# Turning the uint8 codes of x by a transposing DMA in tiles 10 to 15, with the statistics of x one tile further ahead

## The chip, the cores and the metric

The kernel runs on one core of a Trainium2 chip. The metric is the device time of one execution in microseconds (us), the median of several runs. Five engines work side by side: TensorE (PE, matmuls and transposes into PSUM), VectorE (DVE), ScalarE (ACT), GpSimd (POOL), and SyncE (SP), which here only issues transfers. Each takes its own instructions strictly in program order; they meet through semaphores.

## The reference

x has 2 batches of 1024 rows of 2048 floats, the context 2 batches of 2048 by 2048. Cut to what matters:

```python
def fake_quant(x, scale, zp):
    q = clip(round(x / scale + zp), 0, 255)
    return (q - zp) * scale
def attn(x1, x2):                       # x1 = layernorm(x), x2 = ctx
    return matmul(fake_quant(x1, s1, z1), fake_quant(x2, s2, z2))
def lora_moe(f, A, B, Wr):              # 4 experts of rank 16, top 2
    logits = f @ Wr.T
    gates = softmax(keep_top2(logits))
    mid = einsum('tf,erf->ter', f, A)
    return sum_e(gates[e] * (mid[e] @ B[e].T)) * 4.0
x = x + tanh(g_xattn) * attn(layernorm(x), ctx)
x = x + tanh(g_ffn) * lora_moe(layernorm(x), A, B, Wr)
```

## The kernel before

The 2048 rows of x are 16 tiles of 128 rows, numbered 0 to 15 here and in the code. For each tile the kernel does this:

- **Codes of x.** DVE takes mean and variance of x (`stats_x` twice, each two `bn_stats` of 512 columns and each waiting for its half of x from HBM; then `var_x`). POOL raises the variance to -1/2 (`power_x`), DVE makes scale and offset from it (`scale_of_x`), ACT writes the codes as bytes (`scale_x` to `x_byte`). PE turns them in byte pairs, as eight 128x128 transposes of 2-byte values into the PSUM bank `ps_gate` (`turn_q1`); ACT spreads them to fp16 less the zero point (`copy_q1T` to `q1T`, two buffers in turn). In the second batch ACT also sums the codes of each row (`sum_codes`), and DVE makes a correction of the sum (`shift_of_row`).
- **Main product.** `main(b, n)` is 16 matmuls of 128x128 by 128x512 for quarter n of the 2048 columns. DVE adds each quarter to x (`add_main`, which gives x1) and takes its statistics (`stats_h`, then `var_h`, POOL's `power_h`, DVE's `bias_h`). There are two PSUM banks for the quarters, so that main(b, 1) waits until `add_main(b-1, 3)` has emptied its bank.
- **Second layer norm, in two fp16 parts.** ACT writes the high part of h (`high_part`) and h itself (`normal_half` twice), POOL the low part (`low_part` twice). Both parts are turned, and PE multiplies them with A and Wr (`mid_hi` twice, `mid_lo` twice). In tiles 8 to 13 (`MOVED`) the turning is done by SP with transposing transfers of 128x1024 fp16 (`move_hi`, `move_lo`), in the others by PE.
- **Gates and delta.** DVE ranks the four logits (`rank_gates`, which waits for the last `mid_lo`), ACT takes the exponentials (`gate_exp`), DVE makes the gated products (`weigh`), PE turns them into `ps_gate` (`turn_gate`), DVE splits them into two parts (`split_gate`), and PE makes the four quarters of delta, two matmuls each (`delta`). DVE adds them (`add_delta`), SP stores the rows.

Each engine's order is written out by hand up to tile 8. From tile 9 (`STEADY`) on a loop over b runs on each engine. Iteration b holds the main product of tile b, the second layer norm of tile b-1, and gates and delta of tile b-2. For x the loop before works on tile b+1. The last instructions ahead of the loop are those of tile 8's third and fourth quarter and of the gates of tile 7.

x lies in a ring of five tiles. `load_x(b+3)` is issued when tile b-2 is stored. The lines of the four `load_x` of tiles 10 and 11 stand just ahead of the loop on SP, behind the stores of tile 6.

Of the kernel before, what the change touches and what calls it, by code (L numbers as in the profile page):

```python
# [11 lines left out]
F16 = mybir.dt.float16  # L12
I32 = mybir.dt.int32
U8 = mybir.dt.uint8

P = 128
BANK = 512
# [10 lines left out]
RING = 5  # L28
FIRST = 4
STEADY = 9  # L30

MOVED = range(STEADY - 1, 14)
UNITS = 18
# [4 lines left out]
def build(nc, x, ctx_in, params, lora_a, lora_b, out):  # L38
# [21 lines left out]
    with ExitStack() as stack:  # L60
# [3 lines left out]
        def sem(name):  # L64
            return stack.enter_context(nc.semaphore(name))
# [141 lines left out]
        h_bias_ready, h2_ready, h_hi_ready, h_lo_ready = sem("h_bias_ready"), sem("h2_ready"), sem("h_hi_ready"), sem("h_lo_ready")  # L207
        hi_turned, hiT_ready = sem("hi_turned"), sem("hiT_ready")
        lo_turned, loT_ready = sem("lo_turned"), [sem("loT_ready0"), sem("loT_ready1")]
        hi_moved, lo_moved = [sem("hi_moved0"), sem("hi_moved1")], [sem("lo_moved0"), sem("lo_moved1")]  # L210
        last_hi = sem("last_hi")
        hi_used, lo_used, mids_read, mids_scaled = sem("hi_used"), sem("lo_used"), sem("mids_read"), sem("mids_scaled")
# [18 lines left out]
        def half(h):  # L231
            return slice(h * HALF, (h + 1) * HALF)
# [28 lines left out]


        loT = q1T[:, 3, :, :].rearrange("p (h k) m -> p h k m", h=2)
        c_byte = c_code[:, :, :].rearrange("p s n -> p (s n)").bitcast(U8).rearrange("p (s n two) -> p s n two", s=2, two=2)[:, :, :, 0]
        q2_byte = q2[:, 1, :, :].rearrange("p k n -> p (k n)").bitcast(U8).rearrange("p (k n two) -> p k n two", k=KT, two=2)
        q2_pair = q2[:, 1, :, :].rearrange("p k n -> p (k n)").bitcast(F32).rearrange("p (k n) -> p k n", k=KT)
# [10 lines left out]
        def _(sp):  # L277
# [27 lines left out]
            def move_hi(b, h):  # L305
                sp.wait_ge(h_hi_ready, b + 1)
                sp.wait_ge(hi_used, 2 * (b - 1) + h + 1)
                sp.wait_ge(lo_used, 2 * turned(b))
                sp.dma_start_transpose(hT[:, h, :, :], h_hi[:, half(h)]).then_inc(hi_moved[h], 16)

            def move_lo(b, h):
                sp.wait_ge(h_lo_ready, 4 * b + 2 * h + 2)
# [78 lines left out]
            load_x(11, 1)  # L391
            for b in range(STEADY, TILES):
                if b - 1 in MOVED:
                    move_hi(b - 1, 0)
                    move_hi(b - 1, 1)
                    move_lo(b - 1, 0)
                    store(b - 2, 0)
                    move_lo(b - 1, 1)
                    store(b - 2, 1)
                else:  # L400
                    for h in range(2):
                        store(b - 2, h)
                if b + 3 < TILES:
                    load_x(b + 3, 0)
                    load_x(b + 3, 1)
# [10 lines left out]
        def _(pool):  # L416
# [14 lines left out]
            def power_x(b):  # L431
                pool.wait_ge(x_var_ready, b + 1)
                nc.gpsimd.tensor_tensor(x_rstd[:, :], x_var[:, :], half_neg[:, :], ALU.pow).then_inc(x_rstd_ready, 1)  # L433
# [81 lines left out]
            power_h(7)  # L515
            low_part(7, 0)
            low_part(7, 1)
            for b in range(STEADY, TILES):
                power_h(b - 1)
                low_part(b - 1, 0)  # L520
                if b < LAST:
                    power_x(b + 1)
                low_part(b - 1, 1)
            power_h(LAST)


        @block.scalar
        def _(act):
# [16 lines left out]

            def scale_x(b):
                act.wait_ge(q_scale_ready, b + 1)
                wait(act, q1_turned, b)
                wait(act, codes_summed, 2 * (b - PER_B))
                nc.scalar.activation(x_byte[:, :], xr[:, b % RING, :], ACT.Identity,  # L550
                                     bias=q_scale[:, 1:2], scale=q_scale[:, 0:1]).then_inc(x_scaled, 1)
# [8 lines left out]
                                         accum_out=code_sums[:, h:h + 1]).then_inc(codes_summed, 1)  # L560

            def copy_q1T(b):
                act.wait_ge(q1_turned, b + 1)
                if b >= FIRST:
                    last_user = {FIRST: 0, FIRST + 1: 2}.get(b, b - 2)
                    act.wait_ge(main_done, parts_done(last_user, NB - 1))
                nc.scalar.activation(q1T_of(b).rearrange("p (j two) m -> p j two m", two=2),  # L567
                                     as16(turn_bank(b), U8).rearrange("p (j m two) -> p j two m", m=P, two=2),
                                     ACT.Identity, bias=neg_centre[:, 0:1], scale=1.0).then_inc(q1T_ready, 1)

            def high_part(b):
# [144 lines left out]
            for b in range(STEADY, TILES):  # L716
                if b > STEADY:
                    gate_exp(b - 2)
                high_part(b - 1)
                normal_half(b - 1, 0)  # L720
                normal_half(b - 1, 1)
                if b - 1 not in MOVED:
                    copy_hiT(b - 1, 0)
                    copy_hiT(b - 1, 1)
                if b < LAST:
                    scale_x(b + 1)
                if b - 1 not in MOVED:
                    copy_loT(b - 1)
                if b < LAST:
                    copy_q1T(b + 1)  # L730
                    sum_codes(b + 1)
                else:
                    gate_exp(b - 1)

# [13 lines left out]
        def _(pe):  # L748
# [152 lines left out]
            def program(general):  # L901
# [284 lines left out]
                for b in range(STEADY, TILES):  # L1186
                    main(b, 0, general)
                    if b == STEADY:
                        delta(b - 2, 0)
                        delta(b - 2, 1)  # L1190
                    main(b, 1, general, 0, 6)
                    if b > STEADY:
                        turn_gate(b - 2, b + 1)
                    main(b, 1, general, 6, 12)
                    if b > STEADY:
                        delta(b - 2, 0)
                        delta(b - 2, 1)
                    main(b, 1, general, 12)
                    if b - 1 not in MOVED:
                        turn_hi(b - 1, 0)  # L1200
                        turn_hi(b - 1, 1)
                    main(b, 2, general, 0, 10)
                    delta(b - 2, 2)
                    delta(b - 2, 3)
                    main(b, 2, general, 10, 12)
                    mid_hi(b - 1, 0)
                    if b - 1 not in MOVED:
                        turn_lo(b - 1, 0)
                    main(b, 2, general, 12)
                    mid_hi(b - 1, 1)  # L1210
                    if b - 1 not in MOVED:
                        turn_lo(b - 1, 1)
                    main(b, 3, general, 0, 2)
                    if b < LAST:
                        turn_q1(b + 1, b - 1)
                    main(b, 3, general, 2, 6)
                    if b - 1 not in MOVED:
                        mid_lo(b - 1, 0)
                        mid_lo(b - 1, 1)
                    main(b, 3, general, 6, 14)  # L1220
                    if b - 1 in MOVED:
                        mid_lo(b - 1, 0)
                        mid_lo(b - 1, 1)
                    main(b, 3, general, 14)
                    if b - 1 not in MOVED:
                        turn_gate(b - 1, TILES)
                delta(LAST - 1, 0)
                delta(LAST - 1, 1)
                pe.wait_ge(x1_ready, NB * LAST + 3)
# [9 lines left out]
                mid_lo(LAST, 0)  # L1239
                mid_lo(LAST, 1)  # L1240
                keep_busy(10)
                turn_gate(LAST, TILES)
                last_delta()

            with pe.If_ne(flag, 0):
# [8 lines left out]
        def _(dve):  # L1254
# [406 lines left out]
            add_main(8, 2)  # L1661
            weigh(7)
            stats_h(8, 2)
            for b in range(STEADY, TILES):
                if b > STEADY:
                    rank_gates(b - 2)
                else:
                    split_gate(b - 2)
                add_main(b - 1, 3)
                stats_h(b - 1, 3)  # L1670
                var_h(b - 1)
                if b > STEADY:
                    weigh(b - 2)
                bias_h(b - 1)
                if b < LAST:
                    stats_x(b + 1, 0)
                add_main(b, 0)
                if b > STEADY:
                    split_gate(b - 2)
                else:  # L1680
                    add_delta(b - 2, 0)
                shift_of_row(b)
                stats_h(b, 0)
                if b < LAST:
                    stats_x(b + 1, 1)
                    var_x(b + 1)
                if b > STEADY:
                    add_delta(b - 2, 0)
                add_delta(b - 2, 1)
                add_main(b, 1)  # L1690
                if b < LAST:
                    scale_of_x(b + 1)
                add_delta(b - 2, 2)
                add_delta(b - 2, 3)
                stats_h(b, 1)
                if b - 1 not in MOVED:
                    copy_loT(b - 1)
                add_main(b, 2)
                if b == LAST:
                    rank_gates(b - 1)  # L1700
                stats_h(b, 2)
                if b == LAST:
                    weigh(b - 1)
            split_gate(LAST - 1)
# [50 lines left out]
```

## Time and profile before

| what | value |
|---|---|
| median of 3 runs | 349.45 us (349.28 to 350.9) |
| the profiled execution | 350.64 us, of which its span is 348.9 us |
| PE busy | 321.4 us, 92% |
| DVE busy | 276.0 us, 79% |
| granted clock of TensorE | 1.00 of full speed |
| ACT busy | 252.2 us, 72% |
| POOL busy | 109.5 us, 31% |
| 52 loads of ctx, 32 of x | 14.8 us and 6.2 us from issue to landing (median) |

The span is the time from the first instruction to the last in the profiled execution. All starts are microseconds from its beginning. The busy share is a mean over a first part (to about 190 us, with the load of ctx beside it), the loop (iterations 9 to 15, about 199 to 325 us) and a tail. Times of PE come in two forms: the timeline gives when an instruction starts, the chain of waits when it takes over from the one before it, which is some 0.16 us later for matmuls in a row.

### The profile page before, as it was taken

What the parts mean: (1) busy time and instruction counts of PE and PEld (TensorE: products, weight loads), DVE (VectorE), ACT (ScalarE), POOL (GpSimd) and SP (SyncE); (2) the same over time, 40 slices, a digit from 0 to 9 for tenths busy, and PEclk for the clock granted to TensorE, in tenths of its full rate; (3) what the DMA queues carried; (4) which work ended last, traced back from release to release, by engine and by line L of the source; (5) the groups of instructions that cost most, each with busy time, mean ns of one, the idle gap of its engine ahead of it and who ended that gap; (6) DMA issues with size and microseconds to landing.
All of it is one profiled execution on the core that took longest, in us unless ns stands there. A gap on an engine that the chain in (4) does not pass through costs nothing.

```text
span 348.9 us, 6112 instructions
## 1 busy us (share of the span) xinstructions
PE 321.4 (92%) x2180; PEld 175.4 (50%) x2180; DVE 276.0 (79%) x695; ACT 252.2 (72%) x221; POOL 109.5 (31%) x123
## 2 busy tenths in 40 slices
PE   0389999999999999998999999999999999999884
PEld 0134444446675555544656546454545454556452
DVE  4798789988779869865877985969797887965885
ACT  1699899999999999888999347565565656566050
POOL 3100243226656270244235042232415050505000
PEclk9999999999999999999999999999999999999999
DMA  6999999931389858967330777464949491822023
GB/s 207 416 417 421 418 421 417 420 123 45 137 287 365 321 174 267 333 223 245 144 120 16 235 234 224 128 204 138 213 140 191 153 174 69 168 75 111 11 119 124
DMA packets 44528, 75.45 MB, mean 216 GB/s; under 512 B 27600, under 2 KB 27600, under 8 KB 44368
## 3 DMA queue, kind: packets, MB, share of 16 engines
q1 hardware_dynamic: 44496, 75.02, 63.3%
q8 instruction: 20, 0.33, 0.3%
q14 instruction: 12, 0.10, 0.1%
HBM read 51.94 MB, written 16.78 MB: 197 GB/s over the span
## 4 chain that ended last, share of the span: by engine, by line
PE 62%; DVE 14%; DMA 12%; issue 4%; ACT 3%; SPq 3%; POOL 1%; DVEq 0%; ACTq 0%; POOLq 0%
PE ps_main L785 32%; DMA out_x<-xr 5%; DMA xr<-in_x 4%; PE ps_delta L785 4%; PE ps_mid L844 4%; DMA q<-in_ctx 4%; PE ps_delta L874 3%; PE ps_turn L785 3%; PE ps_delta L876 3%; DVE xr L1360 3%; DVE small_tile L1304 2%; PE ps_mid L785 2%; PE ps_gate L785 2%; PE ps_mid L855 2%; PE ps_turn L829 2%
## 5 line engine op out<-in xcount | busy, mean ns | idle before, releaser
L785 PE MATMUL ps_main<-q,q1T 128*128 128x512 f16 x832 | 201.9, 379 | 2.8 <-DVE xr L1360 2.0
L785 PEld LDWEIGHTS ps_main<-q,q1T 128*128 128x128 f16 x832 | 76.1, 98 | 84.4 <-issue 8.6
L450 POOL TENSOR_TENSOR h_parts<-work,h_parts 128x512 f16<-128x512 f32 x30 | 34.2, 1161 | 54.4 <-ACT work L587 54.4
L581 ACT ACTIVATE h_parts<-xr,small_tile 128x2048 f16<-128x2048 f32 x15 | 31.4, 2091 | 25.7 <-DVE small_tile L1377 24.8
L550 ACT ACTIVATE x_byte<-xr,small_tile 128x2048 uint8<-128x2048 f32 x16 | 33.4, 2089 | 20.1 <-DVE small_tile L1319 20.1
L1304 DVE BATCH_NORM_STATS2 small_tile<-xr 128x6 f32<-128x512 f32 x64 | 40.8, 681 | 8.5 <-DMA xr<-in_x 8.5
L543 ACT ACTIVATE c_code<-q,small_tile 128x1024 uint8<-128x1024 f32 x32 | 38.1, 1237 | 9.2 <-DMA q<-in_ctx 8.6
L1365 DVE BATCH_NORM_STATS2 small_tile<-xr 128x6 f32<-128x512 f32 x64 | 43.7, 687 | 0.8
L1360 DVE SCALAR_TENSOR_TENSOR xr<-ps_main,small_tile,xr 128x512 f32<-128x512 f32 x52 | 38.5, 741 | 3.4 <-PE ps_main L785 3.4
L438 POOL TENSOR_TENSOR small_tile<-small_tile 128x1 f32<-128x1 f32 x16 | 8.8, 551 | 89.1 <-DVE small_tile L1373 89.1
L450 POOL TENSOR_TENSOR h_parts<-q1T,h_parts 128x512 f16<-128x512 f32 x30 | 34.3, 1164 | 2.1 <-ACT q1T L587 2.1
L874 PE MATMUL ps_delta<-lora_bT,gT_hi 128*128 128x512 f32 x60 | 30.0, 500 | 0.9 <-DVE gT_hi L1425 0.4
L567 ACT ACTIVATE q1T<-ps_gate,small_tile 128x2048 f16<-128x2048 uint8 x12 | 23.6, 1963 | 5.7 <-PE ps_gate L768 5.6
L433 POOL TENSOR_TENSOR small_tile<-small_tile 128x1 f32<-128x1 f32 x16 | 9.4, 590 | 51.0 <-DVE small_tile L1311 51.0
L756 PE MATMUL ps_main<-ident_h 128*128 128x512 f16 x47 | 13.3, 433 | 12.6 <-issue 12.6
L543 ACT ACTIVATE q<-q,small_tile 128x1024 uint8<-128x1024 f32 x20 | 24.5, 1238 | 0.0
L876 PE MATMUL ps_delta<-lora_bT,gT_lo 128*128 128x512 f32 x60 | 24.4, 406 | 0.0
L1437 DVE SCALAR_TENSOR_TENSOR xr<-ps_delta,small_tile,xr 128x512 f32<-128x512 f32 x30 | 21.2, 745 | 3.8 <-PE ps_delta L876 3.2
L1291 DVE TENSOR_SCALAR q<-c_code,small_tile 128x1024 f16<-128x1024 f16 x32 | 20.5, 647 | 3.7 <-ACT c_code L543 3.5
L1434 DVE TENSOR_TENSOR xr<-ps_delta,xr 128x512 f32<-128x512 f32 x32 | 21.5, 682 | 1.5 <-PE ps_delta L876 1.3
L844 PEld LDWEIGHTS ps_mid<-a_parts,hT 128*128 128x128 f16 x256 | 17.3, 98 | 7.1 <-issue 1.0
L456 POOL MEMSET q<- 128x1024 f32 x16 | 15.1, 955 | 18.1 <-ACT q L543 9.3
(134 smaller groups left out, 463.5 us busy)
## 6 DMA issues: line engine op xcount, KB each, us to landing
q<-in_ctx SPq DMA_DIRECT2D x52, 512.0 KB, 14.8
xr<-in_x SPq DMA_DIRECT2D x32, 512.0 KB, 6.2
out_x<-xr SPq DMA_DIRECT2D x30, 512.0 KB, 3.9
c_code<-in_ctx SPq DMA_DIRECT2D x6, 512.0 KB, 6.5
q1T<-in_ctx SPq DMA_DIRECT2D x6, 512.0 KB, 5.7
h_parts<-in_B SPq DMA_DIRECT2D x1, 1024.0 KB, 17.8
out_x<-xr SPq DMA_DIRECT2D x4, 256.0 KB, 2.3
xr<-in_A SPq DMA_DIRECT2D x1, 544.0 KB, 16.6
```

The costliest lines, as they stand in the source:

```text
L450: nc.gpsimd.tensor_tensor(h_lo[:, half(h)][:, part], work[h][:, part], h_hi[:, half(h)][:, part], ALU.subtract).then_inc(h_lo_ready, 1)
L543: nc.scalar.activation(byte, stage(i), ACT.Identity, bias=par[:, 3:4], scale=inv_s[:, 1:2]).then_inc(row_scaled, 1)
L550: nc.scalar.activation(x_byte[:, :], xr[:, b % RING, :], ACT.Identity, bias=q_scale[:, 1:2], scale=q_scale[:, 0:1]).then_inc(x_scaled, 1)
L567: nc.scalar.activation(q1T_of(b).rearrange("p (j two) m -> p j two m", two=2), as16(turn_bank(b), U8).rearrange("p (j m two) -> p j two m" ...
L581: nc.scalar.activation(h_hi[:, :], xr[:, b % RING, :], ACT.Identity, bias=h_bias[:, b % 2:b % 2 + 1], scale=h_rstd[:, b % 2:b % 2 + 1]).th ...
L785: mm = pe.matmul(product_bank(b, n)[:, :], q1T_of(b)[:, k, :], q2[:, batch(b), slot(batch(b), k), cols(n)], start=(k == 0), stop=(k == KT ...
L844: mm = pe.matmul(ps_mid[:, 0:2 * J], hT[:, h, k, :], a_parts[:, kk, :, :].rearrange("p c j -> p (c j)"), start=(kk == 0), stop=False)
L874: pe.matmul(ps_delta[n % 2][:, :], gT_hi[:, :], lora_bT[:, cols(n)], start=True, stop=False)
L876: pe.matmul(ps_delta[n % 2][:, :], gT_lo[:, :], lora_bT[:, cols(n)], start=False, stop=True).then_inc(delta_done, 1)
L1304: nc.vector.bn_stats(x_stats[:, n, :], xr[:, b % RING, cols(n)]).then_inc(x_stats_done, 1)
L1360: nc.vector.scalar_tensor_tensor(out=x1, in0=product_bank(b, n)[:, :], scalar=gain[:, 0:1], in1=x1, op0=ALU.mult, op1=ALU.add).then_inc(x1 ...
L1365: nc.vector.bn_stats(h_stats[:, b % 2, n, :], xr[:, b % RING, cols(n)]).then_inc(h_stats_done, 1)
```

## The change

- PE no longer turns the codes of tiles 10 to 15. SP turns them with one transposing transfer each (`move_codes`) of `x_byte`, read as 128x1024 two-byte values, into the buffer `c_code`, which is free by then. It is the first of SP's transfers in iterations 9 to 14, ahead of `move_hi`. ACT's `copy_q1T` reads from there instead of from PSUM.
- The statistics of x go one tile further ahead on DVE: both `stats_x` and `var_x` of tile b+2 stand at the end of iteration b, and those of tile 10 ahead of the loop. POOL's `power_x` follows.
- `scale_of_x(b+1)` is now at the start of DVE's iteration, ahead of `rank_gates` and `add_main(b-1, 3)` (in iteration 9 behind `split_gate(7)`), and `scale_x(b+1)` is ahead of `high_part` on ACT. `sum_codes` and `copy_q1T` change places.
- On PE `turn_gate(b-2)` stands four matmuls later, the second `mid_lo` behind the last two matmuls of the main product.

```diff
+MOVED_CODES = range(STEADY + 1, 16)
+        x_turned = c_code[:, 0, :].bitcast(U16).rearrange("p (j m) -> p j m", m=P)
+            def move_codes(b):
+                sp.wait_ge(x_scaled, b + 1)
+                sp.wait_ge(row_scaled, 4 * KT)
+                wait_q1T(sp, b - 1)
+                sp.dma_start_transpose(x_turned, x_byte[:, :].bitcast(U16)).then_inc(q1_moved, 16)
                 if b - 1 in MOVED:
+                    move_codes(b + 1)
                     move_hi(b - 1, 0)
...
             low_part(7, 1)
+            power_x(STEADY + 1)
             for b in range(STEADY, TILES):
                 power_h(b - 1)
                 low_part(b - 1, 0)
-                if b < LAST:
-                    power_x(b + 1)
                 low_part(b - 1, 1)
+                if b < LAST - 1:
+                    power_x(b + 2)
...
                 if b > STEADY:
                     gate_exp(b - 2)
+                if b < LAST:
+                    scale_x(b + 1)
                 high_part(b - 1)
                 normal_half(b - 1, 0)
                 normal_half(b - 1, 1)
...
-                if b < LAST:
-                    scale_x(b + 1)
...
                 if b < LAST:
+                    sum_codes(b + 1)
                     copy_q1T(b + 1)
-                    sum_codes(b + 1)
...
-                    main(b, 1, general, 0, 6)
+                    main(b, 1, general, 0, 10)
                     if b > STEADY:
-                        turn_gate(b - 2, b + 1)
-                    main(b, 1, general, 6, 12)
+                        turn_gate(b - 2, MOVED_CODES[0])
+                    main(b, 1, general, 10, 12)
...
                     main(b, 3, general, 0, 2)
-                    if b < LAST:
-                        turn_q1(b + 1, b - 1)
                     main(b, 3, general, 2, 6)
...
                     main(b, 3, general, 6, 14)
                     if b - 1 in MOVED:
                         mid_lo(b - 1, 0)
+                    main(b, 3, general, 14)
+                    if b - 1 in MOVED:
                         mid_lo(b - 1, 1)
-                    main(b, 3, general, 14)
...
             stats_h(8, 2)
+            stats_x(STEADY + 1, 0)
+            stats_x(STEADY + 1, 1)
+            var_x(STEADY + 1)
             for b in range(STEADY, TILES):
+                if b == STEADY:
+                    split_gate(b - 2)
+                if b < LAST:
+                    scale_of_x(b + 1)
                 if b > STEADY:
                     rank_gates(b - 2)
-                else:
-                    split_gate(b - 2)
                 add_main(b - 1, 3)
                 stats_h(b - 1, 3)
                 var_h(b - 1)
                 if b > STEADY:
                     weigh(b - 2)
                 bias_h(b - 1)
-                if b < LAST:
-                    stats_x(b + 1, 0)
                 add_main(b, 0)
...
                 stats_h(b, 0)
-                if b < LAST:
-                    stats_x(b + 1, 1)
-                    var_x(b + 1)
...
                 add_main(b, 1)
-                if b < LAST:
-                    scale_of_x(b + 1)
...
                 stats_h(b, 2)
+                if b < LAST - 1:
+                    stats_x(b + 2, 0)
+                    stats_x(b + 2, 1)
+                    var_x(b + 2)
```

## Rows read from the trace of the kernel before

**Rows 1.** The chain that ended last, iterations 12 and 13: start, us, what.

```profile
267.75 0.45 PE ps_gate L768 x8
...
284.12 0.86 PE ps_main L785 x4
...
285.88 0.45 PE ps_gate L768 x8
...
288.92 0.51 PE ps_mid L855 x16
```

**Rows 2.** Timeline of PE, iterations 13 and 15: start, us, line, out<-in.

```profile
276.31 0.27 PE L866 MATMUL ps_gate<-ident_f,gated 128*128 128x128 f32 x1
...
278.59 0.40 PE L874 MATMUL ps_delta<-lora_bT,gT_hi 128*128 128x512 f32 x1
...
312.55 0.27 PE L866 MATMUL ps_gate<-ident_f,gated 128*128 128x128 f32 x1
...
314.43 0.39 PE L874 MATMUL ps_delta<-lora_bT,gT_hi 128*128 128x512 f32 x1
```

**Rows 3.** Timeline of DVE, iteration 13, and one row of iteration 15.

```profile
271.32 0.31 DVE L1390 TENSOR_REDUCE ps_mid<-ps_mid 128x68 f32<-128x136 f32 x1 [2.65 <-PE ps_mid L855]
...
275.75 1.27 DVE L1304 BATCH_NORM_STATS2 small_tile<-xr 128x6 f32<-128x512 f32 x2
276.94 0.73 DVE L1360 SCALAR_TENSOR_TENSOR xr<-ps_main,small_tile,xr 128x512 f32<-128x512 f32 x1
277.59 0.28 DVE L1425 CAST gT_hi<-ps_gate 128x128 fp32r<-128x128 f32 x1
...
279.09 1.27 DVE L1304 BATCH_NORM_STATS2 small_tile<-xr 128x6 f32<-128x512 f32 x2
280.50 0.27 DVE L1309 BATCH_NORM_AGGREGATE small_tile<-small_tile 128x2 f32<-128x24 f32 x1
...
282.87 0.20 DVE L1316 TENSOR_SCALAR small_tile<-small_tile 128x1 f32<-128x1 f32 x1
...
283.42 1.40 DVE L1437 SCALAR_TENSOR_TENSOR xr<-ps_delta,small_tile,xr 128x512 f32<-128x512 f32 x2
...
312.86 0.29 DVE L1425 CAST gT_hi<-ps_gate 128x128 fp32r<-128x128 f32 x1
```

**Rows 4.** Line 282 (load_x), window 196 to 197: the two loads of tile 10.

```profile
L282 SPq DMA_DIRECT2D xr<-in_x x2: 432/576/719, 195.7 to 196.2; - x2
...
DMA to landing us min/median/max: 5.5/6.3/7.0
```

**Rows 5.** Timeline of DVE around the start of iteration 9.

```profile
198.16 0.69 DVE L1365 BATCH_NORM_STATS2 small_tile<-xr 128x6 f32<-128x512 f32 x1
...
199.79 0.75 DVE L1360 SCALAR_TENSOR_TENSOR xr<-ps_main,small_tile,xr 128x512 f32<-128x512 f32 x1
...
201.71 0.15 DVE L1373 TENSOR_SCALAR small_tile<-small_tile 128x1 f32<-128x1 f32 x1
202.53 0.21 DVE L1377 TENSOR_SCALAR small_tile<-small_tile 128x1 f32<-128x1 f32 x1 [0.66 <-POOL small_tile L438]
```

**Rows 6.** Timeline of POOL, iteration 9.

```profile
201.94 0.55 POOL L438 TENSOR_TENSOR small_tile<-small_tile 128x1 f32<-128x1 f32 x1 [10.20 <-DVE small_tile L1373]
```

**Rows 7.** Timeline of PE, iteration 9.

```profile
203.97 5.79 PE L785 MATMUL ps_main<-q,q1T 128*128 128x512 f16 x26
...
210.98 0.64 PE L844 MATMUL ps_mid<-a_parts,hT 128*128 128x136 f16 x8
```

**Rows 8.** Timeline of SP, and line 315 (move_lo) over the whole loop.

```profile
204.90 2.67 SPq L309 DMA_TRANSPOSE hT<-h_parts  x2
...
211.15 1.25 SPq L315 DMA_TRANSPOSE q1T<-h_parts  x1
...
284.23 1.25 SPq L315 DMA_TRANSPOSE q1T<-h_parts  x1
...
DMA to landing us min/median/max: 2.7/2.7/4.4
```

More of the change, by code:

```diff
@@ L14 @@
 U8 = mybir.dt.uint8
+U16 = mybir.dt.uint16
 P = 128
@@ L209, in build @@
         lo_turned, loT_ready = sem("lo_turned"), [sem("loT_ready0"), sem("loT_ready1")]
+        q1_moved = sem("q1_moved")
         hi_moved, lo_moved = [sem("hi_moved0"), sem("hi_moved1")], [sem("lo_moved0"), sem("lo_moved1")]
@@ L547, in scale_x @@
                 act.wait_ge(q_scale_ready, b + 1)
-                wait(act, q1_turned, b)
+                if b - 1 in MOVED_CODES:
+                    act.wait_ge(q1_moved, 16 * (b - MOVED_CODES[0]))
+                else:
+                    wait(act, q1_turned, b)
                 wait(act, codes_summed, 2 * (b - PER_B))
@@ L562, in copy_q1T @@
             def copy_q1T(b):
-                act.wait_ge(q1_turned, b + 1)
+                if b in MOVED_CODES:
+                    act.wait_ge(q1_moved, 16 * (b - MOVED_CODES[0] + 1))
+                    turned_codes = c_code[:, 0, :].bitcast(U8)
+                else:
+                    act.wait_ge(q1_turned, b + 1)
+                    turned_codes = as16(turn_bank(b), U8)
                 if b >= FIRST:
@@ L567, in copy_q1T @@
                 nc.scalar.activation(q1T_of(b).rearrange("p (j two) m -> p j two m", two=2),
-                                     as16(turn_bank(b), U8).rearrange("p (j m two) -> p j two m", m=P, two=2),
+                                     turned_codes.rearrange("p (j m two) -> p j two m", m=P, two=2),
                                      ACT.Identity, bias=neg_centre[:, 0:1], scale=1.0).then_inc(q1T_ready, 1)
@@ L1222, in program @@
                         mid_lo(b - 1, 0)
+                    main(b, 3, general, 14)
+                    if b - 1 in MOVED:
                         mid_lo(b - 1, 1)
-                    main(b, 3, general, 14)
                     if b - 1 not in MOVED:
-                        turn_gate(b - 1, TILES)
+                        turn_gate(b - 1, MOVED_CODES[0])
                 delta(LAST - 1, 0)
@@ L1241, in program @@
                 keep_busy(10)
-                turn_gate(LAST, TILES)
+                turn_gate(LAST, MOVED_CODES[0])
                 last_delta()
```

## The prediction

> **What bounds the kernel now.** I read the cores and the clock first (full speed all through, so a matmul costs the same before and after), then the chain of waits over the loop, then the timelines of PE, DVE, POOL and SP of one iteration side by side. The chain repeats with a period of 285.88 - 267.75 = 18.13 us [rows 1]. PE has almost no gap in it, but it isn't free of waiting. From `turn_gate` to the second of the deltas behind it iteration 13 takes 278.59 - 276.31 = 2.28 us, and iteration 15, where DVE has no statistics of x in its way, takes 314.43 - 312.55 = 1.88 us for the same work [rows 2]. So 0.40 us of each period is a wait for `split_gate` on DVE.
>
> For the sums I name three moments of an iteration. **T** is the start of `main(b, 0)`: 288.92 + 0.51 + two matmuls at 0.86/4 each = 289.86 for iteration 14, so 271.73 for iteration 13. **D** is the end of `main(b, 2)`, 284.12 + 0.86 = 284.98 [rows 1]. **R** is the start of `rank_gates`, 271.32, which is T - 0.41 [rows 3]. From T to D PE needs 13.25 us, 12.85 of it work; from D to the next T 4.88 us.
>
> **What goes from PE.** The eight transposes take 0.45 us in each of iterations 9 to 14 [rows 1], on the engine that sets the period: six times, 2.7 us in all. D to T becomes 4.43.
>
> **What moves on DVE: the steady iteration.** The x statistics leave the stretch between `bias_h` and `add_main(b, 0)`. That takes 276.94 - 275.75 = 1.19 us out of the way of the gates: the cast of `split_gate` comes at R + 6.27 now and at R + 5.08 after [rows 3]. But R itself can no longer be early, because `rank_gates` now stands behind `scale_of_x(b+1)`, and that behind a chain that begins at D. Step by step:
>
> - `add_main(b, 2)` and `stats_h(b, 2)`: 0.75 + 0.69 [rows 5], to D + 1.44.
> - Four `bn_stats` and on to the aggregate: 280.50 - 279.09 = 1.41 for two, plus 1.19 for two more [rows 3], to D + 4.04. The aggregate is 0.27 long; with its gap 0.3, to D + 4.34.
> - DVE to POOL 201.94 - 201.71 = 0.23, POOL and back 202.53 - 201.94 = 0.59 [rows 5, 6], to D + 5.16. POOL's `low_part` is done well before.
> - `scale_of_x`: 283.42 - 282.87 = 0.55 [rows 3], to R = D + 5.71.
>
> The next T is at D + 4.43, so R = T + 1.28, where it was T - 0.41. The second delta can start 278.59 - 277.59 = 1.00 us after the cast [rows 2, 3], at R + 6.08 = T + 7.36. PE alone would be there at T + 4.58 (276.31 - 271.73) + 1.88 = T + 6.46. So the wait is 0.90 instead of 0.40, and the new period 12.85 + 0.90 + 4.43 = 18.18 us, 0.05 more than before. The 0.45 taken from PE comes back as waiting for DVE. Bounds: each of the five handovers in the chain may be off by some 0.03, which puts R within 0.15 and the five periods within 0.75 us in all. The addition of main's last quarter, also later, ends at R + 2.1 and holds up `main(b, 1)` at most until T + 3.4, which is no more than its place.
>
> `turn_gate` stands closer to the deltas: in iteration 15 the cast follows it by 312.86 - 312.55 = 0.31 [rows 2, 3], the second delta by 1.31, and four matmuls fewer lie between, 1.88 - 0.86 = 1.02. That is a floor of 0.29 us under the wait, hidden under the 0.90 in the middle, but paid in iteration 15, which had no wait.
>
> **What moves on DVE: the entry of the loop.** `stats_x(10)` now stands right behind `stats_h(8, 2)`, which starts at 198.16 [rows 5]. The halves of tile 10 are issued at 195.7 and 196.2 and land 5.5 and 7.0 us later, at 201.2 and 203.2 [rows 4]; before, both were read later. DVE, in order, stands still until 203.2. Queued behind it are `split_gate(7)`, for which the deltas of tile 7 wait, and `add_main(8, 3)`, for whose bank `main(9, 1)` waits. From 203.2: 1.41 and 0.3 to the end of `var_x`, 205.0; POOL 0.23 + 0.59, 205.8; `scale_of_x(10)` 0.55, 206.35; `add_main(8, 3)` 0.75, 207.1. `split_gate(7)` fits under POOL (cast at 205.05, the deltas end about 206.5). `main(9, 1)` starts at 207.1 instead of 203.97 [rows 7]: 3.15 us lost.
>
> Tile 8's second norm is later still, by 206.35 - 199.79 = 6.56 [rows 5]. `move_hi(8, 0)` goes out at 204.90 + 6.56 = 211.46 and lands by 214.2 [rows 8]; `mid_hi(8, 0)` is due at 210.98 + 3.15 = 214.13 [rows 7]. Another 0.1. `move_lo(8, 1)` goes out at 211.15 + 6.56 less 0.5, as `power_x` no longer stands between POOL's two low parts (0.55 [rows 6]): 217.2. Landing takes 2.7 to 4.4 [rows 8], so 219.9 to 221.6, and the second `mid_lo` is due 4.0 after D, about 219.75. 0.15 to 1.85 us; below 0.6 it only takes from the wait at the next deltas, so it costs 0 to 1.2. I take 0.1, since the same transfer lands in 2.7 in the median row.
>
> **The new transfer.** The trace shows no move of codes; the nearest row is `move_lo`, of the same 128x1024 two-byte values: 1.25 us of SP's time and 2.7 to 4.4 to land [rows 8]. `scale_x` would end about R + 3.2 and `copy_q1T` come at about R + 11, so both ends are hidden, by 3 us at least; uncovered, it would be its landing less 0.45. On SP only `move_hi` is queued behind it, and `h_hi` is ready at about R + 6.7, when the 1.25 us have passed. ACT reads SBUF instead of PSUM in `copy_q1T`; 0 to 0.15 us, hidden by the same slack. `move_lo(b-1, 1)` goes out at 284.23 - 271.32 - 0.5 = R + 12.4, D - 0.05, and has 4.0 us until it is needed: at 4.4 it makes PE wait 0.35, which the delta's wait gives back.
>
> The worst landing deserves a thought. In these rows a move that stands behind a store lands in up to 4.4 us. The Trainium skill (DMA: Bandwidth & Descriptors, Queues, rings and completion order) says that the write to the semaphore lands only after every earlier write from that DMA engine. By it the codes would be reported only after the loads of x issued ahead of them; with the slack above the sum stays the same, and only the third rival below gains by it.
>
> **Sum.** Entry 3.15 + 0.1 + 0.1; five periods, D of iteration 9 to D of 14, at 0.05: 0.25; last, D of 14 onward, -0.45 + 0.29 = -0.16. Together +3.45 us. The span goes from 348.9 to 352.4, the profiled execution from 350.64 to 354.1. The median of the runs is 1.2 below the profiled execution, which I keep: 349.45 + 3.45 = 352.9 us, 1% slower.
>
> **Rivals.** 0.5%, 1.75 us, is about what a measurement of this kernel can tell from no change.
> 1. *The steady chain is shorter than I make it.* If R came at T + 0.66 or earlier, only the floor of 0.29 would stay, and each period would be 17.57. For it: 0.6 us over eight instructions. Against: DVE's spacing repeats to hundredths. Five periods save 2.8 in place of losing 0.25: 349.9 us, no change. Chance 0.15.
> 2. *Faster: PE alone decides.* The DVE wait for tile 10 is the point from which it decides: if the second half lands before 200.1 us, 3.1 earlier than in the trace, so that the 3.9 us from there to the end of `add_main(8, 3)` are over by 203.97, and the steady chain is short too, neither `split_gate(7)` nor the ranks are late, and 6 x 0.45 + 5 x 0.11 - 0.29 = 2.96 are saved: 346.5 us. Against it stand [rows 4]. Chance 0.08.
> 3. *Transfers hold each other up.* One more transposing transfer per tile, and loads issued 1 to 2 us later; if `move_lo` then took 5.5 instead of 2.7 to 4.4, the excess would no longer fit under the delta's wait, some 0.4 us a tile, and the entry would cost 1.1 more: 352.9 + 2.0 + 1.1 = 356.0 us. For it: landings of 4.4 in the later iterations. Chance 0.17.
> My forecast, both parts as computed (351.5 to 354.5): 0.55; the remaining 0.05 lies between it and no change.
>
> So faster 0.09, same 0.18, slower 0.73. The range leaves out the second rival and reaches to the other two: 349.7 to 356.1 us.
>
> **What would show it.** In the new profile: DVE idle before L1304 at about 199 to 203, put down to the loads of x; `main(9, 1)` near 207; a period of 18.1 to 18.3; `rank_gates` about 1.3 us after T, with an idle stretch before `scale_of_x` put down to POOL's power; PE waiting for the cast of `split_gate` by 0.9 us. It is wrong if the loads of tile 10 land earlier, if the period is 17.6, or if `mid_lo` or `mid_hi` wait for a transfer by more than 0.4 us.

## The result, and the profile after

| | median | ratio to the kernel before, 95% interval |
|---|---|---|
| before | 349.37 us (four runs; the table before the prediction has three of them) | |
| changed | 356.02 us (355.08 to 357.2) | 1.0182 [1.0153, 1.0211] |

The change makes the kernel 1.8% slower: 6.65 us by the medians, where 3.45 were forecast. The profiled execution takes 355.08 us with a span of 353.3. In it the start of the loop lies 1.27 us earlier than before (`turn_gate(7)` at 197.56 against 198.83), a difference that the first part makes by itself. From `turn_gate(7)` to the end the changed kernel needs 155.7 us, the kernel before 150.1: 5.7 us of loss are in the traces. The remaining 1 us between that and the medians I can't assign; the interval of the ratio, in time 5.3 to 7.4 us, holds the 5.7, so it need not be more than the spread of the runs.

**The entry.** DVE's timeline of the changed kernel (start, us, line, in brackets the idle time before it), to be laid beside [rows 5]:

```profile
200.53 1.29 DVE L1325 BATCH_NORM_STATS2 small_tile<-xr 128x6 f32<-128x512 f32 x2 [2.96 <-DMA xr<-in_x]
202.06 1.29 DVE L1325 BATCH_NORM_STATS2 small_tile<-xr 128x6 f32<-128x512 f32 x2 [0.24 <-DMA xr<-in_x]
...
203.87 0.29 DVE L1446 CAST gT_hi<-ps_gate 128x128 fp32r<-128x128 f32 x1
...
205.17 0.74 DVE L1381 SCALAR_TENSOR_TENSOR xr<-ps_main,small_tile,xr 128x512 f32<-128x512 f32 x1
...
207.91 0.21 DVE L1398 TENSOR_SCALAR small_tile<-small_tile 128x1 f32<-128x1 f32 x1 [0.66 <-POOL small_tile L451]
```

DVE stands still for tile 10's loads, and `split_gate(7)` and `add_main(8, 3)` come behind them. PE's timeline of the changed kernel, beside [rows 7]:

```profile
204.22 0.50 PE L896 MATMUL ps_delta<-lora_bT,gT_hi 128*128 128x512 f32 x1 [2.28 <-DVE gT_hi L1446]
...
205.97 6.82 PE L807 MATMUL ps_main<-q,q1T 128*128 128x512 f16 x26
...
214.92 0.65 PE L866 MATMUL ps_mid<-a_parts,hT 128*128 128x136 f16 x8 [0.75 <-DMA hT<-h_parts]
```

`main(9, 1)` starts at 205.97 instead of 203.97. With the 1.27 us that is 3.27 us lost. But the same 26 matmuls now take 6.82 us instead of 5.79, and behind them PE waits 0.75 us for a transfer. The windows of the changed kernel (in each row: the stretch, its length, busy time of PE, of PE's weight loads, of DVE, ACT and POOL, then the granted clock, the DMA's busy share, GB/s) show the first of the two:

```profile
202.00:204.20 2.20, 0.00 (x0) 0.00 (x0) 1.93 (x6) 0.00 (x0) 0.18 (x1) 1.00 0.52 212
204.20:206.00 1.80, 1.78 (x5) 0.94 (x6) 1.61 (x6) 0.71 (x1) 0.37 (x1) 0.64 0.00 0
206.00:208.00 2.00, 2.00 (x6) 0.70 (x6) 1.16 (x4) 1.38 (x1) 0.55 (x1) 0.50 0.00 0
208.00:210.00 2.00, 2.00 (x10) 0.90 (x9) 1.96 (x6) 1.84 (x1) 0.00 (x0) 0.97 0.58 131
```

After PE has stood still, the granted clock reads 0.64 and 0.50, which is the lower level of 1.2 GHz, until about 208 us. That is 6.82 - 5.79 = 1.03 us. (The four deltas ahead of it are slower too, 1.75 us instead of 1.12, but that costs nothing more: `add_main(8, 3)`, for which `main(9, 1)` waits, ends only at 205.91, and in run 5 below, where the clock stays up, `main(9, 1)` starts no earlier.) The second is in SP's timeline and in the landings of line 315 (`move_hi`), window 211 to 212.5, beside [rows 8]:

```profile
210.28 2.58 SPq L315 DMA_TRANSPOSE hT<-h_parts  x2
...
DMA to landing us min/median/max: 4.0/4.3/4.6
```

Both moves of tile 8's high part land late, after 4.6 and 4.0 us instead of 2.7 to 2.8. The view of the DMA queues over 212 to 213.5 us shows what else is in flight:

```profile
DMA  9999999999962100000009157999999999999990
...
q8 instruction: 1, 0.02, 4.0%
```

Queue q8 brings a piece of an engine's program, and the 16 engines are idle for a while in the middle of the second move.

**The steady iterations.** DVE's timeline of the changed kernel, iterations 11 and 12, beside [rows 3]:

```profile
239.74 0.21 DVE L1337 TENSOR_SCALAR small_tile<-small_tile 128x1 f32<-128x1 f32 x1 [0.67 <-POOL small_tile L446]
...
240.30 0.30 DVE L1411 TENSOR_REDUCE ps_mid<-ps_mid 128x68 f32<-128x136 f32 x1
...
245.37 0.28 DVE L1446 CAST gT_hi<-ps_gate 128x128 fp32r<-128x128 f32 x1
...
258.46 0.30 DVE L1411 TENSOR_REDUCE ps_mid<-ps_mid 128x68 f32<-128x136 f32 x1
```

and PE's, beside [rows 2]:

```profile
238.60 0.41 PE L877 MATMUL ps_mid<-a_parts,q1T 128*128 128x68 f16 x8
238.85 5.94 PE L807 MATMUL ps_main<-q,q1T 128*128 128x512 f16 x26
244.72 0.33 PE L888 MATMUL ps_gate<-ident_f,gated 128*128 128x128 f32 x1
...
246.36 0.39 PE L896 MATMUL ps_delta<-lora_bT,gT_hi 128*128 128x512 f32 x1
...
257.53 0.42 PE L877 MATMUL ps_mid<-a_parts,q1T 128*128 128x68 f16 x8 [0.60 <-DMA q1T<-h_parts]
```

The period is 258.46 - 240.30 = 18.16 us (18.13 before). T is 238.85 + 0.16 = 239.01, so `rank_gates` comes at T + 1.29 and the cast 5.07 behind it. The second delta starts at T + 7.35, where PE alone would be there at T + 6.46: it comes 0.89 us late, 0.49 more than the 0.40 before and so more than the 0.45 that the transposes gave back. The last row is a `mid_lo` that waits for its move; it bears on the next period, 18.35 us.

### The profile page after: what moved, and what is told of

Same layout as the page of the kernel before. It is cut to its first block and busy times, and to the rows that moved or that the text cites. A ratio compares the mean times of both kernels' runs of the same rounds, so it can differ in the third digit from the quotient of the medians.

```text
span 353.3 us, 6022 instructions
## 1 busy us (share of the span) xinstructions
PE 322.1 (91%) x2132; PEld 172.3 (49%) x2132; DVE 276.8 (78%) x695; ACT 251.6 (71%) x221; POOL 109.6 (31%) x123
## 5 line engine op out<-in xcount | busy, mean ns | idle before, releaser
L624 ACT ACTIVATE small_tile<-mids,small_tile 128x4 f32<-128x4 f32 x16 | 4.7, 294 | 45.1 <-DVE small_tile L1419 45.1
L866 PE MATMUL ps_mid<-a_parts,hT 128*128 128x136 f16 x256 | 20.4, 223 | 1.5 <-DMA hT<-h_parts 0.7
```

The source lines that it names most:

```text
L866: mm = pe.matmul(ps_mid[:, 0:2 * J], hT[:, h, k, :], a_parts[:, kk, :, :].rearrange("p c j -> p (c j)"), start=(kk == 0), stop=False)
```

## The experiments

Each was timed in five rounds beside the kernel before on the same chip. Its ratio is to that kernel.

**1. The entry as before.** Tile 10's statistics, scaling and turning go as in the kernel before, all else as changed.

```diff
-MOVED_CODES = range(STEADY + 1, 16)
+MOVED_CODES = range(STEADY + 2, 16)
...
-            stats_x(STEADY + 1, 0)
-            stats_x(STEADY + 1, 1)
-            var_x(STEADY + 1)
...
                 bias_h(b - 1)
+                if b == STEADY:
+                    stats_x(b + 1, 0)
...
```

> Iteration 9 and tile 10 go as in the kernel before (statistics of x where they were, codes turned by PE); the statistics of tiles 11 to 15 one tile ahead and their codes by transfer, as in the changed kernel. If most of the loss is made at the entry, where DVE waits for tile 10's loads, the time falls from 356.0 to about 349.7 us: the entry's 5.2 us gone, 4 periods of 18.16 to 18.3 instead of 18.13 (+0.1 to +0.7), the last tile -0.16. Rival, that the loss lies in the steady iterations or in the transfers of codes in each of them: not below 353.

350.5 us, ratio 1.0006 [0.9982, 1.003]. The whole measurable loss is made at the entry, and the steady part, with five of the six transfers, is neither gain nor loss within the 0.2% of the interval.

**2. Scale behind rank.**

```diff
-                if b < LAST:
+                if b == STEADY:
                     scale_of_x(b + 1)
                 if b > STEADY:
                     rank_gates(b - 2)
+                    if b < LAST:
+                        scale_of_x(b + 1)
                 add_main(b - 1, 3)
```

> The changed kernel, but from iteration 10 on DVE makes scale_of_x(b+1) behind rank_gates(b-2) instead of ahead of it; the entry is left as it is. If the wait of DVE for POOL's power ahead of rank_gates is what gives back the 0.45 us of PE, the period falls from 18.16 to 17.6 us (only the floor of 0.29 stays under the second delta): 356.0 - 5 x 0.57 = 353.1 us. Where a move_lo lands in 4.4 or more, some 0.3 us of that are lost again. Rival, that in the new order the transfers set the period: it stays within 0.2 of 18.16, no gain.

353.53 us, ratio 1.0109 [1.0075, 1.0143], 2.5 us less than the changed kernel. DVE's `rank_gates` in this version:

```profile
238.50 0.31 DVE L1411 TENSOR_REDUCE ps_mid<-ps_mid 128x68 f32<-128x136 f32 x1
...
256.80 0.31 DVE L1411 TENSOR_REDUCE ps_mid<-ps_mid 128x68 f32<-128x136 f32 x1 [0.70 <-PE ps_mid L877]
...
274.37 0.31 DVE L1411 TENSOR_REDUCE ps_mid<-ps_mid 128x68 f32<-128x136 f32 x1
...
291.95 0.31 DVE L1411 TENSOR_REDUCE ps_mid<-ps_mid 128x68 f32<-128x136 f32 x1
```

The last two periods shown are 17.57 and 17.58 us, as worked out for a short chain. The one of 18.30 holds a `mid_lo` that waited for its move.

**3. Both.**

> Entry as in the kernel before and scale_of_x behind rank_gates from iteration 10 on. If the two causes are separate, their gains add: about 4 periods at 17.6 instead of 18.13, the last tile -0.16, the first -0.1, so 349.4 - 2.4 = 347.0 us, faster than the kernel before by 0.7%. Rival (transfers as the next bound): 348.5 to 349.4.

348.43 us, ratio 0.9964 [0.9943, 0.9986]: faster than the kernel before, by half of what was expected. In its trace PE waits 1.1 us for `move_lo` (in two places) and 0.3 for `move_hi`.

**4. All codes by PE.** The changed order, without the transfers of codes.

```diff
-MOVED_CODES = range(STEADY + 1, 16)
+MOVED_CODES = range(0)
-                    move_codes(b + 1)
...
                     main(b, 3, general, 0, 2)
+                    if b < LAST:
+                        turn_q1(b + 1, b - 1)
...
```

> The order of the changed kernel on DVE, POOL and ACT, but PE turns all codes of x as before and no transfer of codes is made. By my reasoning the 0.45 us of PE that comes back lies under the wait for DVE: period 12.85 + 0.45 + 4.88 = 18.18 us against 18.16, so 356.0 us as the changed kernel, within 0.7. If the mid_hi waits of the changed kernel come from the added transfer, about 1 us less. Rival, that PE's work sets the period: 6 x 0.45 more, 358.7 us.

355.96 us, ratio 1.0185 [1.0152, 1.0217], the same as the changed kernel. DVE's `rank_gates` come at 239.38 and 257.54, a period of 18.16 with the transposes back on PE:

```profile
239.38 0.30 DVE L1412 TENSOR_REDUCE ps_mid<-ps_mid 128x68 f32<-128x136 f32 x1
257.54 0.30 DVE L1412 TENSOR_REDUCE ps_mid<-ps_mid 128x68 f32<-128x136 f32 x1
```

So in the changed order the transfers, which are what the change is about, are worth nothing that can be measured. PE's 0.45 us lies under DVE's chain in both. The equal medians hide one difference: in this run `move_hi(8)` lands after 2.8 and 2.7 us and its wait at the entry is gone, and from `turn_gate(8)` to the end the trace is 0.3 us longer than that of the changed kernel (127.1 against 126.8).

**5. Matmuls into the stand-still.**

```diff
                     if b == STEADY:
+                        pe.wait_ge(out_ready, NB * (b - 2))
+                        for _ in range(10):
+                            pe.matmul(ps_delta[0][:, :]..., ident_h[:, :], ident_h..., start=True, stop=True)
                         delta(b - 2, 0)
```

> The changed kernel with ten extra matmuls on the identity (2.2 us, into a free bank) at the place where PE stands still 2.28 us for split_gate(7). Nothing else moves. In the changed kernel the granted clock then reads 0.64 and 0.50 for some 3.8 us, and main(9, 1) and its neighbours take about 1 us longer. If the stand-still is what takes the clock down, it stays at 1.00 and the run is 1 us faster than the changed kernel: 355.0. Rival, that the clock falls for another reason: 356.0, clock as before.

354.05 us, ratio 1.0116 [1.008, 1.0152]: 2 us less, where 1 was expected. The clock stays at 1.00 in the windows, and the mean clock of all six executions is 0.997 or more, where that of three of the four of the changed kernel is 0.993 to 0.995; `main(9, 1)` and what follows take 5.79 us again, and `move_hi(8)` lands in 2.7 and 2.8 us, so that its wait of 0.75 goes too. That second part had not been thought of. More instructions on PE had also moved the q8 packet, to between 207 and 208 us, ahead of the move. So this run alone doesn't separate the two. In the trace the entry, from `turn_gate(7)` to `turn_gate(8)`, shrinks by 1.4 us (29.0 to 27.6) and not by the whole 1.9 of clock and late move, because the second `mid_lo` of tile 8, which had no wait in the changed kernel, now waits 0.47 us for its own move.

**6. Tile 10's loads ahead of the stores of tile 6.**

```diff
+            load_x(10, 0)
+            load_x(10, 1)
             store(6, 0)
             store(6, 1)
-            load_x(10, 0)
-            load_x(10, 1)
```

> The changed kernel with the two loads of tile 10 issued ahead of the stores of tile 6 (about 193.5 instead of 195.7 us of the span, and with no store ahead of them in the queue). If the landing of tile 10 is what costs the 3.27 us and, through the clock, 1.03 more, both go: main(9, 1) starts when it did. What stays is that the statistics come ahead of add_main(8, 3), 3.3 us for tile 8's second norm, so that mid_hi(8) and mid_lo(8) may wait 0 to 2 us. Expected 351.3 us, 350.6 to 352.6. Rival, that the order of instructions and not the loads makes the loss: over 354.

353.12 us, ratio 1.009 [1.006, 1.012]: 3 us gained, but 1.8 short of the middle of the expectation. DVE waits 0.82 us for the loads instead of 3.2, PE's stand-still is gone, the clock stays up. PE's timeline shows the rest:

```profile
204.47 5.79 PE L807 MATMUL ps_main<-q,q1T 128*128 128x512 f16 x26 [0.46 <-DVE xr L1381]
...
213.37 0.65 PE L866 MATMUL ps_mid<-a_parts,hT 128*128 128x136 f16 x8 [1.74 <-DMA hT<-h_parts]
```

**7. The last, and scale behind rank.**

> As the last, and with scale_of_x behind rank_gates from iteration 10 on: 2.5 to 3 us less than the last, 348.6 us. All six tiles' codes are moved by transfer here. If it is not faster than the version with the entry as before (0.9964 of the kernel before), the late second norm of tile 8 costs what the sixth transfer saves.

351.37 us, ratio 1.0035 [1.0004, 1.0065]. The repair of the steady part brings 1.8 us here. The wait of `mid_hi(8)` is 1.7 us again, and the version is slower than run 3, which leaves tile 10 alone: bringing tile 10 forward costs more than its transfer saves. But most of the 2.5 us between the two ratios is that wait, and runs 9 to 12 tie it to the place of a q8 packet and not to the order as such.

**8. Run 3 with the stores behind both moves of the low part.**

```diff
                     move_lo(b - 1, 0)
-                    store(b - 2, 0)
                     move_lo(b - 1, 1)
+                    store(b - 2, 0)
```

> The version with both repairs, and both moves of the low part ahead of the stores on SP. In the trace of that version the second mid_lo waits for its move twice (1.1 us in all of PE's time, 2.1 of its weight loads) and mid_hi once (0.3). If a store ahead of the second move makes it land late, these waits go and the time falls by about 1 us to 347.4. Rival, that the landing varies for another reason: no change, 348.4.

347.79 us, ratio 0.9951 [0.9923, 0.9979], the fastest version. In its trace no `mid` waits for a move in PE's own time, and the periods are 17.73, 17.58, 17.71, 17.57, 17.58. Against run 3 (0.9964) the difference lies inside the intervals, so that the order of stores and moves is not shown to be the reason.

**9 to 12. Where the q8 packet falls.** Run 9 is run 6 with 48 waits on a semaphore that is long reached, in `main(9, 0)`; run 10 puts them into the changed kernel; run 11 is run 6 with the waits behind the moves; run 12 has them only in the copy of PE's loop that isn't executed.

```diff
-                    main(b, 0, general)
+                    for k in range(KT):
+                        main(b, 0, general, k, k + 1)
+                        if b == STEADY:
+                            for _ in range(3):
+                                pe.wait_ge(consts_ready, 2)
```

> The version with tile 10's loads earlier, and on PE 48 waits on a semaphore that is long reached, three behind each matmul of main(9, 0). They cost PE's queue little and move nothing else, but everything PE fetches of its program after them comes some 3 to 5 us earlier in time. In the trace of that version a 16 KB packet of program (queue q8) falls at about 211 us into the flight of tile 8's move_hi, which then lands in 4.0 and 4.6 instead of 2.7 us, and mid_hi waits 1.7 us. If the packet is the cause, the moves of iteration 9 land in 2.7 to 2.9, that wait goes, and the time is 1.7 us less than 353.1: 351.4. Rival, that the moves land late because of the order of transfers: 4.0 and 4.6 as before, 353.1.

351.41 us, ratio 1.0043 [1.001, 1.0075]. The wait of 1.7 us is gone, as expected, though the second `mid_lo` now waits 0.54. The ratio's interval overlaps those of runs 6 and 12, so that it is the trace and not the time that shows the gain (from `turn_gate(7)` to the end 151.4 us, 153.0 in that of run 6). Line 315 over iteration 9 of this run, where the packet falls between 205 and 206 us, ahead of both moves:

```profile
L315 SPq DMA_TRANSPOSE hT<-h_parts x2: 1233/1240/1247, 207.3 to 208.7; - x2
...
DMA to landing us min/median/max: 2.7/2.7/2.7
```

> The same 48 waits in the changed kernel as it is. Its mid_hi(8) waits 0.75 us with a packet of program at 212.7. If the packet is the cause: 0.75 us less than 356.0, 355.3, the clock still falling to 0.50 behind the stand-still (1 us). Rival: 356.0 with the same landings.

355.01 us, ratio 1.0134 [1.0086, 1.0183], the landings 2.7 and 2.8 as expected. In the trace the clock does not do what was expected:

```profile
202.00:204.20 2.20, 0.08 (x1) 0.00 (x0) 1.82 (x5) 0.00 (x0) 0.04 (x1) 1.00 0.53 214
204.20:206.00 1.80, 1.17 (x4) 0.71 (x4) 1.61 (x6) 0.57 (x1) 0.51 (x1) 1.00 0.00 0
206.00:208.00 2.00, 1.89 (x9) 0.89 (x10) 1.17 (x4) 1.53 (x1) 0.54 (x1) 1.00 0.04 8
```

PE stands still for 2.48 us, no less than in the changed kernel, and the clock doesn't fall. This execution is the exception, however: its mean clock is 0.998 and its time 353.35 us, while the other five have mean clocks of 0.994 or 0.995, as the changed kernel has, and times of 354.4 to 357.6. The median, 355.01, is close to the 355.3 that was expected with the clock falling.

> Control to the first of these: the same 48 waits, but in main(9, 3), behind the moves of tile 8's high part. The packet of about 211 us stays where it is: move_hi lands in 4.0 and 4.6, mid_hi waits 1.7 us, 353.1 us. If the 48 waits themselves help or cost, it shows here.

352.89 us, ratio 1.0075 [1.0049, 1.0102]. Not the control it was meant to be: the packet did move, to between 208 and 209 us, at the very start of the first move, and the moves land in 2.9 and 2.7 us. The 48 waits in a row cost PE 0.6 us, and a `mid_lo` waited 0.9.

> Repair of the control, whose extra waits shifted the packet of program too (to 208.3 us), since PE's program holds two copies of the loop and only the second is executed: whatever is added to the first moves the second in memory. Here the version with tile 10's loads earlier gets 48 waits in the first copy alone. Not one executed instruction changes. If a packet of program inside a transposing transfer makes it land late, the packet moves from 211.0 to about 208.3 us, tile 8's move_hi lands in 2.7 to 2.9 us instead of 4.0 and 4.6, mid_hi's wait of 1.7 us goes, and the time is 351.4 to 352.4. Rival, that the executed waits of the earlier runs did it: 353.1, landings of 4.0 and 4.6.

352.95 us, ratio 1.0068 [1.0042, 1.0095]. The premise was wrong: the copy that isn't executed doesn't shift the packet, which comes 2.2 us behind the issue of the first move, as in run 6. With it stay the late landings (4.0 and 4.6) and the wait (1.73). As a repetition of run 6 it is a fair control to run 9.

The landings of `move_hi(8)` (first and second move) and the place of the packet, in the changed kernel and in every run that brings tile 10 forward as it does:

| version | first move issued, us | q8 packet, us | landings, us |
|---|---|---|---|
| changed | 210.28 | 212 to 213 | 4.6, 4.0 |
| 2 | 210.17 | 212 to 213 | 4.6, 4.0 |
| 6 | 208.76 | 210 to 211 | 4.6, 4.0 |
| 7 | 207.59 | 209 to 210 | 4.5, 4.0 |
| 12 | 208.83 | 211 to 212 | 4.6, 4.0 |
| 4 | 210.43 | 205 to 206 | 2.8, 2.7 |
| 5 | 210.35 | 207 to 208 | 2.7, 2.8 |
| 9 | 207.33 | 205 to 206 | 2.7, 2.7 |
| 10 | 210.41 | 207 to 208 | 2.7, 2.8 |
| 11 | 208.30 | 208 to 209 | 2.9, 2.7 |

Five times the packet falls 2.2 to 2.5 us behind the first issue, and both moves land late. Five times it lies elsewhere, and none does.

The same holds for all 405 transposing transfers in the traces of the two kernels and the twelve runs. 267 of them have no packet of program at all, of q8 or of the smaller ones of q14, from 1.5 us before their issue to 3.3 us after it; none of these lands after more than 3.65 us. 60 land after 3.7 us or more, and every one of them has a 16 KB packet that starts between 1 us before its issue and 3 us after. And the late landing sits, at first, on one DMA engine: a transfer reports by 16 increments of its semaphore, and for the first `move_hi(8)` of the changed kernel 15 of them come 2.60 to 2.71 us after the issue and the last after 4.60. So it is in all five late rows of the table. For the second move all 16 are late.

## Why the prediction was right in kind and short in size

- **The wait for tile 10's loads: right.** 3.15 us forecast at `main(9, 1)` (its terms add up to 3.06, the rest is rounding upwards on the way), 3.27 in the trace. The second cause of lateness in that sum, `scale_of_x` ahead of `add_main(8, 3)`, showed as worked out (cast to addition 1.30 us). Run 6 gives the price from the other side: with the loads earlier, that start is late by 0.8 us only, counted from `turn_gate(7)` (204.47 - 198.54 against 203.97 - 198.83).
- **What follows at the entry: mis-sized, the step that fails.** I took 0.1 for `mid_hi(8)`, 0.1 for `mid_lo(8)`, and nothing for the clock, since it was at full speed all through the kernel before. The trace has 1.03 us of slower matmuls and 0.91 us for the late move, 0.75 of them idle. The 0.1 for `mid_hi(8)` came from taking the median landing of 2.7 for a move that had no slack left, although [rows 8] had shown 4.4. I had looked for a store as the reason for a late landing, and no store was near. `mid_lo(8)` doesn't wait in the changed kernel, but waits 0.47 to 0.54 us in runs 5, 9 and 10, where `mid_hi(8)` is in time. The price of the clock was not in the sum because nothing in it asked what a stand-still of PE does to the clock. From `turn_gate(7)` to the `mid_hi(8)` wait's end, 17.36 us against 12.15 before, 5.21 where I had 3.25.
- **From the profiled execution to the median: wrong.** I kept the 1.2 us by which the median of the kernel before lay below its profiled execution. The changed kernel's median lies 0.9 above its own. The profiled execution was forecast at 354.1 and took 355.08, the median at 352.9 and is 356.02: two thirds of that miss is this step. It is no larger than the spread between executions, and nothing in the traces ties it to the change.
- **The steady iteration: right, to a few hundredths.** `rank_gates` at T + 1.29 (1.28 forecast), wait 0.89 (0.90), period 18.16 (18.18). Run 4 shows that the transfers give nothing in this order, run 2 that it is `scale_of_x` ahead of the ranks that eats the gain: the floor of 0.29 under the wait and the period of 17.57 came out too. Over all five periods the trace has 0.61 us of loss, not 0.25: two of them, 18.35 and 18.39, hold a `mid_lo` and a `mid_hi` whose moves landed late, the others are 18.15 to 18.17. That the delta's wait gives a late `move_lo` back held for the most part: PE waited 0.60 us for one at 257.5, and that period is 18.35 (276.81 - 258.46), 0.19 longer.
- **The last tile: right,** -0.17 against -0.16.
- **The rivals.** The short steady chain and the faster kernel did not occur; run 2 is what the first of them would look like. The third, transfers that hold each other up, is true in part: moves landed late, but by all signs not for the order of the kernel's own transfers. The Trainium skill (DMA: Bandwidth & Descriptors, Queues, rings and completion order) states its rule, that a semaphore write lands only after every earlier write from its DMA engine, across the queues of that engine. No store or load stood ahead of `move_hi(8)`, but by that rule a packet of q8 would hold it up just as well, and the trace agrees as far as it goes: the packet starts 2.54 us behind the issue, when 15 of the 16 increments are in or about to be, and only the last comes late, at 4.60. No run shows that it is this rule and nothing else on that engine.
- **The number: luck.** 356.02 lies 0.1 us inside the range, at the very price of the third rival, which put its upper end at 356.1. That rival's sum was another: 2.0 us for a `move_lo` of 5.5 us in the steady tiles and 1.1 more for `mid_lo` at the entry. In the trace the late moves of the steady tiles cost some 0.4 us in all and `mid_lo(8)` nothing; what fills the gap is the clock, the late `move_hi(8)` and the spread of the executions. (The chances of the rivals add up to 0.08 faster, 0.20 the same and 0.72 slower, each 0.01 or 0.02 off the line below them.)

Of the 6.65 us, then: 3.3 the wait for the loads, 1.0 the clock, 0.9 the late move, 0.6 the steady part, -0.2 the last tile, and 1 us between traces and medians that stays open. Runs 1 and 6 show the first as a cause, and run 2 shows that `scale_of_x` ahead of the ranks is what leaves the steady part without a gain. Run 5, where the clock stays up in all six executions, shows that the stand-still is what takes it down. That the packet of program is the cause of late landings rests on all transposing transfers of the fourteen traces, on the forecasts of runs 9 and 10, whose landings came true, and on runs 11 and 12, where the packet did not go where it was expected to and the landing followed the packet. No run moved the packet and nothing else.

## What to carry to other kernels

Work taken off the bounding engine is worth only what the next chain leaves of it: before such a change, find from the trace by how much the next engine in the ring is late, and place the new early work behind what that ring waits for (here one line, `scale_of_x` behind `rank_gates`, is the difference between 18.16 and 17.57 us a tile). Whoever brings a read of loaded data forward on an engine that works in order must look up when the load lands, at the entry of the loop above all, and what is queued behind the read. A transfer with no slack is to be costed at its worst landing, not its median.

## What the runs showed of the hardware that I had not expected

- A transposing transfer of 128x1024 two-byte values lands in 2.7 to 2.8 us (203 of the 267 that no packet of program comes near, the others in up to 3.65), but in 4.2 to 4.6 in all 21 cases in which a 16 KB piece of an engine's program (queue q8) starts 1.6 to 2.2 us behind its issue. In the kernel before, the four moves that land after 3.9 us or more have such a packet too; the `move_lo` issued at 284.23 us, which landed in 4.4, has it 1.6 us behind. It follows that instructions added on PE, which moved the packet in runs 5, 9, 10 and 11 (but not in run 12, where they are never executed), can make or end a wait of up to 1.7 us that has nothing to do with what they do.
- After a stand-still of PE of 2.3 to 2.4 us the granted clock went to the lower level (1.2 GHz) for some 3 us in the traces of the changed kernel and of runs 2 and 4, and cost 1.0 us in the changed kernel; in run 10's trace it did not, after 2.48 us. Over all executions of these four versions, 19 of 22 have a mean clock of 0.995 or less, against 5 of 100 of the other versions and 6 of 90 of the kernel before. So the fall is what mostly happens, but not always. One of the three exceptions, an execution of the changed kernel with a mean clock of 1.000, took 356.93 us all the same: the spread between executions is as large as the price of the clock. What decides whether it falls was not found.
